# Cross attention's key transfers issued by GpSimd instead of SyncE

## The reference, cut to what matters

```python
q = split_heads(norm(x) @ Wq + bq)            # 512 queries a batch, 16 or 32 heads
k, v = split_heads(ctx @ Wk + bk), split_heads(ctx @ Wv + bv)   # 77 keys
s = q @ k.T * scale
s = where(mask, NEG, s)                       # three of the four kinds are masked
x = x + merge_heads(softmax(s) @ v) @ Wo
```

## Time and profile before

| | |
|---|---|
| median of 3 runs | 2164.26 us (2155.38 to 2170.29) |
| profiled execution | 2162.4 us, span 2160.7 us |
| PE busy | 1858.7 us (86%) |
| DVE busy | 1431.7 us (66%) |
| ACT busy | 1069.5 us (50%) |
| POOL busy | 667.5 us (31%) |
| key transfers | 224 issues of 19.5 KB |

### The profile page before, as it was taken

The page is one execution under the profiler, slowest core; times in us unless marked ns, Lnnn a source line. Parts: engine busy times, 40 slices in busy tenths (PEclk is TensorE's granted clock), DMA queues, the critical chain, the costliest instruction groups (busy, mean ns, idle before and its releaser), DMA issues.

```text
span 2160.7 us, 34572 instructions
## 1 busy us (share of the span) xinstructions
PE 1858.7 (86%) x12971; PEld 1139.4 (53%) x12971; DVE 1431.7 (66%) x3427; ACT 1069.5 (50%) x1523; POOL 667.5 (31%) x903
## 2 busy tenths in 40 slices
PE   5988998584777888898899898999989989999978
PEld 4557665364544444565544564644455544456556
DVE  8667666553677777864677874577785567787564
ACT  2645655131453465564466565366656356656410
POOL 3121112403524353310554320355330244531120
PEclk9979998587787799999999999999999999999987
DMA  6442343121000000141000042000023000013100
GB/s 223 110 128 98 101 108 91 52 79 38 20 1 13 1 1 13 37 110 38 15 1 1 10 109 66 16 1 2 1 74 97 1 16 1 2 31 100 41 5 15
DMA packets 80746, 100.91 MB, mean 47 GB/s; under 512 B 31462, under 2 KB 46190, under 8 KB 79940
## 3 DMA queue, kind: packets, MB, share of 16 engines
q1 hardware_dynamic: 78532, 94.50, 15.6%
q0 software_dynamic: 2048, 4.20, 0.7%
HBM read 52.43 MB, written 12.38 MB: 30 GB/s over the span
## 4 chain that ended last, share of the span: by engine, by line
PE 40%; DVE 15%; ACT 6%; issue 5%; POOL 2%; SPq 1%; DMA 1%; DVEq 0%; POOLq 0%; ACTq 0%
PE wide L839 27%; PE acc L839 12%; DVE maxima L1786 6%; ACT prob L2022 3%; DVE hid L1277 1%; DMA masked_q<-q_g 1%; DVE moments L1322 1%; ACT prob L1945 1%; DVE hn L1374 1%; DVE qkv L1754 1%; POOL rstd L2086 1%; DVE hid L1453 1%; SPq L763 1%; ACT hn L1910 1%; DVE hn L1376 0%
## 5 line engine op out<-in xcount | busy, mean ns | idle before, releaser
L1786 DVE TENSOR_REDUCE maxima<-wide 128x2 f32<-128x512 f32 (+3 forms) x512 | 406.0, 818 | 146.7 <-PE wide L839 144.0
L2022 ACT ACTIVATE prob<-wide 128x768 f32<-128x768 f32 (+1 forms) x384 | 332.2, 881 | 149.0 <-PE wide L839 148.7
L1945 ACT ACTIVATE prob<-wide 77x1024 f32<-77x1024 f32 x256 | 258.1, 1018 | 106.6 <-PE wide L839 106.1
L839 PE MATMUL wide<-q_g 32*128 32x256 f32 (+3 forms) x2048 | 269.0, 395 | 36.2 <-ACT prob L2022 17.8
L2254 POOL TENSOR_SCALAR_AFFINE_SELECT prob<-prob 128x256 f32<-128x256 f32 (+1 forms) x384 | 187.9, 493 | 337.3 <-ACT prob L2022 336.2
L1462 DVE TENSOR_REDUCE maxima<-wide 128x8 f32<-128x616 f32 x256 | 202.8, 795 | 116.9 <-PE wide L839 111.4
L2086 POOL TENSOR_TENSOR rstd<-moments,cst 128x4 f32<-128x4 f32 x88 | 89.7, 1020 | 525.9 <-DVE moments L1350 278.6
L839 PEld LDWEIGHTS wide<-q_g 32*128 32x128 f32 x2048 | 140.6, 189 | 206.5 <-issue 101.6
L1866 ACT ACTIVATE q_g<-wide 128x1024 fp32r<-128x1024 f32 x128 | 131.2, 1025 | 183.9 <-PE wide L839 183.9
L1866 ACT ACTIVATE q_g<-acc 128x512 fp32r<-128x512 f32 x192 | 114.5, 596 | 163.6 <-PE acc L839 157.8
L839 PE MATMUL wide<-kx,q_g 128*128 128x312 f32 x512 | 180.0, 417 | 8.2 <-DVE maxima L1462 6.2
(11 more groups left out here) (247 smaller groups left out, 3036.4 us busy)
## 6 DMA issues: line engine op xcount, KB each, us to landing
masked_q<-q_g SPq DMA_DIRECT2D x448, 64.0 KB
masked_q<-mask_l SPq DMA_DIRECT2D x84, 308.0 KB
masked_k<-kx SPq DMA_DIRECT2D x224, 19.5 KB, 1.8
A<-in_w SPq DMA_DIRECT2D x2, 2048.0 KB, 12.4
unit_w<-in_unit_w SPq DMA_DIRECT2D x8, 448.0 KB, 3.8
ffn_w<-in_ffn_w SPq DMA_DIRECT2D x4, 768.0 KB, 4.8
slots_in<-v_third SPq DMA_DIRECT2D x1, 2560.0 KB, 12.7
prob<-slots_in SPq DMA_DIRECT2D x8, 320.0 KB, 3.2
```

Source lines behind the costliest of these rows:

```text
L839: return e.matmul(out, lhsT, rhs, start=start, stop=stop, is_transpose=turn)
L1786: e.tensor_reduce(top[:, t, h], v[:, :, at0:at0 + P * t + P], AX.X, ALU.max, negate=True).then_inc(*made("max", *([("free", tile)] if t == ...
L1945: e.activation(p[0:SC, :], s[0:SC, :], ACT.Exp, bias=0.0, scale=1.0).then_inc(*made("exp", pb, ("free", tile)))
L2022: e.activation(pv, sv, ACT.Exp, bias=0.0, scale=8 ** -0.5).then_inc(*made("exp", pb, ("free", tile)))
```

## The change

The function `fetch_keys` is taken out of SP's program and put, word for word, into POOL's. The written order stays, so POOL comes to the step where the order has it; the waits are the same, now made by POOL. Queries, masks and weights stay with SP.

```diff
@@ in sync(e)
-            def fetch_keys(n, b, half):
-                ...
-            do = dict(mask_turn=mask_turn, fetch=fetch, fetch_keys=fetch_keys, unit_end=unit_end, ...
+            do = dict(mask_turn=mask_turn, fetch=fetch, unit_end=unit_end, ...
@@ in gpsimd(e)
+            def fetch_keys(n, b, half):
+                tile = ("masked_k", n, b, half)
+                at = T.slot("masked_k", tile)
+                for w in need(T.freed("masked_k", tile), ("kv", n, b), ("masked_ones",)):
+                    e.wait_ge(*w)
+                for i in range(HG):
+                    e.dma_start(masked_k[at][0:HR, :, i, :].bitcast(F32),
+                                kx[HR * i:HR * i + HR, i, 2 * half:2 * half + 2, SK * b:SK * b + SK].bitcast(F32)).then_inc(
+                        *landed(f"fetch_keys{at}", *([tile] if i == HG - 1 else [])))
-                      scatter=scatter, gather=gather, bias_u=bias_u,
+                      scatter=scatter, gather=gather, fetch_keys=fetch_keys, bias_u=bias_u,
```

More of the change, by code:

```diff
@@ L819, in m_store @@
                     *landed(f"out{b}", ("stored", b)))
-            do = dict(mask_turn=mask_turn, fetch=fetch, fetch_keys=fetch_keys, unit_end=unit_end, f0_down=f0_down, f0_hidden=f0_hidden, mask_load=mask_load, extras=extras, masks3=masks3, slots_in=slots_in_,
+            do = dict(mask_turn=mask_turn, fetch=fetch, unit_end=unit_end, f0_down=f0_down, f0_hidden=f0_hidden, mask_load=mask_load, extras=extras, masks3=masks3, slots_in=slots_in_,
                       f1_out=f1_out,
```

## The result

| | before | after |
|---|---|---|
| median | 2171.61 us (2153.26 to 2188.62, 21 runs) | 2154.14 us (2140.1 to 2173.37, 21 runs) |
| ratio | 1 | 0.9939, 95% interval 0.9918 to 0.9960 |
| profiled execution | 2162.4 us, span 2160.7 | 2140.1 us, span 2138.4 |
| PE's waits for queries | 16.5 us, 12 times | 5.1 us, 7 times |

The change made the kernel faster by 0.6%, or 13 us (9 to 18) of the 2171.6. That is within the 1% I had called no difference; 21 runs of each tell it from zero. The ratio is taken from the fast runs alone and is not that of the two medians, which stand 17 us apart. The two profiled executions differ by 22 us.

A forecast was written before the change was run, and what follows sets the result against it. PE in order, busy for 86% of the span, was taken as the bound. Gains of 4.4 + 3.0 + 2.0 = 9.4 us, less 1 for slips, were rounded to 9: 2164.26 - 9 = 2155 us, own range 2149 to 2161.

The forecast's parts named there:

- Units 4 to 7, 4.4 us: Ends of these units' third batches: second mask load and its queries move 1.1 us earlier in each, 4.4 us gained.
- tile 1's data comes 1.1 us earlier and PE still waits some 0.9 us: Last batch of units 4 to 7: tile 0's wait goes, tile 1's shrinks, so each unit gains only 1.1 us.
- rival (C): Nothing gained: queries start earlier but land no earlier, as mask loads fill the DMA engines; 2164 us, chance 0.20.
- rival (D): All 22 us of waits go, queries also travelling faster without the keys' small pieces between them; 2142 us, chance 0.10.
- Unit 0, 3.0 us: Unit 0: queries move 2.0 to 2.5 us earlier, more than each of four waits, so all 3.0 us go.
- Unit 2, 2.0 us: Unit 2: one wait of 2.28 us; its late queries move by 2.0 us at most, 2.0 us gained.
- Unit 1, nothing: Unit 1: its wait of 2.5 us stands behind 3 MB of expert weights, not behind keys, so no gain.
- The 1 us for slips: Deduction of 1 us from the summed gain of 9.4 us for small slips.
- POOL's transfer, 0.96 us: Each key transfer takes POOL 0.96 us, like its indirect ones; a block of four 4.8 us, against gaps of 4.8 to 5.3.
- rival (A): Slower: POOL's plain transfers cost more than 0.96 us, blocks overrun at 12 places and delay DVE; up to 2194 us, chance 0.14.
- Rival (B): Slower: POOL's issues and DVE's small operations keep each other waiting, up to 0.8 us a block; 2177 us, chance 0.06.
- The rule of the Trainium skill: POOL's transfer descriptors cannot be written while DVE holds the shared port; blocks of 7 us, 2175 us in place of 2155.

The follow-up runs named there:

- e1: The changed kernel run again, nothing altered: 0.9927 of the kernel before.
- e12: The changed kernel run once more, on one chip with other versions: 0.9944 of the kernel before.
- e9: The kernel before, with 73 of the 77 mask rows left out of the mask loads in batches 1 to 3: 0.9964 of the kernel before.
- e5: The changed kernel with each key transfer split in two, eight issues a block, same bytes: 0.9949 of the kernel before.
- e6: The changed kernel with each key transfer split in four, sixteen issues a block, same bytes: 1.0551 of the kernel before.
- e7: The changed kernel without the key transfers of batches 1 to 3: 0.9948 of the kernel before.
- e8: The changed kernel with the mask loads issued by POOL too: 0.9976 of the kernel before.
- e4: The kernel before, all keys on SP, with the first half of each batch's keys (half 0) issued one row earlier: 0.9897 of the kernel before.
- e3: The kernel before with only the second half of each batch's keys (half 1) moved to POOL: 1.0007 of the kernel before.
- e10: The kernel before with half 0 of the keys one row earlier on SP and half 1 on POOL: 0.9985 of the kernel before.

## Why the prediction was right, and where a size was off

I forecast 2155 us from 2164, a gain of 9 us, with 0.80 on a change within 1%. It was 13 us (9 to 18), within 1%, and 2154. That 2154 lies so near 2155 is luck: the kernel before stood at 2171.6 in the runs of the result, and not at 2164. The mechanism was the one written down: the next batch's mask loads waited for a block that stood ahead of them, and after it wait for the logits tile. By the steps of the sum:

- **Units 4 to 7, 4.4 us: too small.** PE's waits there fell from 8.7 us to 0.6 in after (0.4 in e1, 2.5 in e12), a gain of 6.2 to 8.3. The second mask load did move by 1.1 us, from 1.12 us behind its tile to 0.03. What failed is the step "tile 1's data comes 1.1 us earlier and PE still waits some 0.9 us": I took the time that a pair travels as fixed. It was 4.5 us, not the "some 5" of rival (C), and fell to 3.7 or less. In e9, with the masks' bytes gone and the block in place, it is 2.4 or less (967.54 to some 969.96), so these bytes were 2 us or more of it. In the changed kernel two things are different for the pair, the wider spacing of the mask loads and the keys' transfers no longer just ahead of them. The second is what rival (D) holds, and no run separates the two.
- **Unit 0, 3.0 us: too large.** The mask loads moved by 2.0 us as worked out, the second from 2.00 us behind its tile to 0.04 (0.26 in e1, 0.38 in e12). The stretch's waits fell from 3.0 to 1.0 in after, 1.5 in e1 and 2.1 in e12: I had taken every wait as shorter than the move. A new one of 0.47 us at the start of the unit comes on top in after.
- **Unit 2, 2.0 us:** its one wait of 2.28 us is gone in all three executions. **Unit 1, nothing:** 2.48 became 3.0 to 3.1.
- **Together:** 11.4 us of waits gone in after, 11.5 in e1, 8.9 in e12, against 9.4 in the sum. The two errors cancel in part, which is luck. The 1 us for slips was about right: the new wait in unit 0 and the longer one in unit 1 took some 1 us together.
- **POOL's transfer, 0.96 us: mis-sized.** It is 0.536. An indirect issue was the wrong neighbour, and the bound from SP, 0.607, was the near one. At 0.96 the block of 4.8 us would by the same sum still have cost nothing, but with 0.0 to 0.5 us of margin; the 0.14 for rival (A) was paid to that doubt. e5 and e6 agree with its turning point and show its price too low: at a block of 7.9 us 133 us more than e5, where it gave 39 at 8.6. It had no term for PE's waits for keys, nor for the clock.
- **Rival (B)** didn't show: of after's 192 small TENSOR_SCALARs on `maxima` 20 overlap a block, as those at 1232.75 and 1234.60 do, and they took 0.18 to 0.28 us. The rule of the Trainium skill, SBUF — State Buffer, § A bandwidth-pool intuition that's wrong (but worth ruling out), which has a transfer of about 620 ns take about 3100 ns while DVE holds the shared port, didn't show either: of 224 issues the longest took 742 ns, and by e7 three quarters of them together cost nothing measurable. Whether any of DVE's operations beside the blocks held that port, no run here shows. **Rival (C)**, that nothing lands earlier, is out by the interval.
- **The clock was in no step.** The sum counts a wait once. In the profiled executions of before, after and ten experiments (all but e6 and e8), units 4 to 7 make 48 stages. In 10 of them PE waited 1.9 us or more for queries: 9 of these ran at a mean granted clock of 0.90 to 0.98, and they lasted 80.9 us on average. Of the other 38, 8 were below 1.00, and the average is 77.1. The difference of 3.8 us (80.9 to 77.1) is more than the difference of the waits, 2.7 us a stage against 0.35. So the gain may pass the sum. Unit 5 of before shows it:

```profile
1299.00:1309.00 10.00, 9.72 (x70) 6.39 (x71) 4.54 (x9) 6.67 (x9) 0.00 (x0) 1.00 0.24 57
1309.00:1319.00 10.00, 7.71 (x53) 4.25 (x50) 6.29 (x23) 5.83 (x8) 1.01 (x1) 0.98 0.60 153
1319.00:1331.00 12.00, 11.49 (x46) 5.04 (x44) 1.49 (x4) 6.16 (x9) 0.00 (x0) 0.59 0.21 51
```

The wait of 2.29 us lies at 1317.47, and behind it the granted clock falls from 1.00 to 0.59, the lower of its two levels (1.2 of 2.4 GHz) for most of the row; PE is busy for 11.5 of 12 us with fewer matmuls than in the row before. In e4, where none of units 4 to 7 waits longer than 0.82 us at one place, all four stages ran at 1.00 and took 76.1 to 76.9 us. But five of the 8 ran below 1.00 without any wait for queries, among them unit 4 of after (0.98) and unit 7 of e5 (0.94), so a wait is not the only thing behind a fall. How many of the 13 us came by the clock stays open: no run held the waits fixed and let the clock alone change.

## What to carry to other kernels

In a queue that waits in order for buffers, look for what stands directly ahead of the transfer that is late: moving that block one row earlier in its own queue gained as much as giving it to another engine. When a block leaves a queue, its transfers lose their place behind the others as well, so move only the part that stood in the way: moving the other half alone gained nothing, and with half 0 on SP it added waits. Before trusting spare time on the receiving engine, double the work there in one run, and again: here the cost was nothing at a block of 3.9 us, under the gap of 5, and 133 us at one of 7.9.

## What was unexpected of the hardware

- A plain SBUF to SBUF transfer of 19.5 KB occupied POOL for 0.536 us and SP for 0.607, and landed after a median of 1.9 and 1.8 us. Split in two or four, an issue took 0.496 us, so half or a quarter of the bytes made it hardly cheaper.
- The same transfers, issued by POOL while mask loads were in flight, lengthened PE's waits for queries from 16.5 to 21.7 us (e3) and from 7.7 to 13.9 (e10), though SP had less to issue. In the changed kernel, where POOL issues both halves, the waits were 5.0 to 7.6 us.
- After a wait of PE of some 2 us the granted clock often stood low for the 10 us and more that followed: 0.59 in unit 5 of before, and 0.50 in unit 7 of e3, behind a wait of 2.55 us at 2024.33. It is no fixed price: in 10 us behind the wait of 2.19 us in unit 7 of before it was 0.92, and behind that of 2.97 us in unit 1 of after it stayed at 1.00. Two stretches of e3, with the columns of the stages:

```profile
2015.00:2025.00 10.00, 7.45 (x48) 3.96 (x48) 5.66 (x20) 5.00 (x7) 3.15 (x5) 0.93 0.61 161
2025.00:2035.00 10.00, 9.74 (x38) 5.25 (x40) 1.51 (x6) 5.82 (x8) 0.00 (x0) 0.50 0.20 48
```
